# Loading and transposing the first layer's output in bf16 through one PSUM tile

## The reference

```python
x = _layernorm(x + attn(x, Ws, Wa, Wo, bo))
up_gate = einsum('bsd,hd->bsh', x, W1);  up_lin = einsum('bsd,hd->bsh', x, W3)   # d = 2048, h = 8192
hidden  = fwht(silu(up_gate) * up_lin)             # Walsh-Hadamard transform over h
x = _layernorm(x + einsum('bsh,dh->bsd', hidden, W2))
```

## Time and profile before

| | us |
|---|---|
| median of 3 timed runs | 6237.64 |
| fastest and slowest of them | 6152.71, 6242.62 |
| the profiled execution, whole | 5735.62 |
| its span on the slowest core (core 4) | 5734.0 |
| spans of the eight cores | 5688.7 to 5734.0 |

### The profile page before, as it was taken

One profiled execution on the slowest core, in us unless ns is written; L12 is line 12 of the kernel. 1 busy time (PEld: TensorE's weight loads), 2 busy tenths in 40 slices (PEclk: granted clock), 3 DMA queues, 4 the chain that ended last, 5 costly groups with the idle time before them and its releaser, 6 DMA issues.

```text
span 5734.0 us, 46561 instructions; the slowest of 8 cores (5688.7 to 5734.0 us)
## 1 busy us (share of the span) xinstructions
PE 3764.7 (66%) x16956; PEld 1737.1 (30%) x17248; DVE 900.4 (16%) x1961; ACT 494.7 (9%) x688; POOL 233.7 (4%) x384
## 2 busy tenths in 40 slices
PE   1211121455665666569999999999995999149980
PEld 0000000112333333334444444444442444014430
DVE  1211121013333332041111011101110000120003
ACT  1111111000111110000000000000000000010002
POOL 0000000210000000000000000000001000000000
PEclk7555565776777778679999999999997999569995
DMA  9888877664222222343223322233224223542224
GB/s 181 144 154 150 149 147 123 112 107 121 78 89 98 87 83 89 119 153 67 57 56 58 61 57 57 56 58 61 58 56 156 88 88 97 174 162 88 90 79 168
DMA packets 295630, 584.28 MB, mean 102 GB/s; under 512 B 18160, under 2 KB 186352, under 8 KB 280560
## 3 DMA queue, kind: packets, MB, share of 16 engines
q0 software_dynamic: 63312, 270.66, 23.8%
q1 hardware_dynamic: 232096, 310.62, 19.2%
HBM read 583.41 MB, written 167.77 MB: 131 GB/s over the span
## 4 chain that ended last, share of the span: by engine, by line
PE 57%; DMA 27%; DVE 5%; issue 4%; SPq 4%; ACT 1%; another core or an unknown queue 1%; POOL 1%; DVEq 0%; ACTq 0%; POOLq 0%
PE up L649 15%; PE up L660 15%; PE dps L760 13%; DMA vc<-vb 7%; DMA t2sb<-w2tmp 5%; PE av L490 4%; PE sc L558 4%; SPq L256 3%; DMA w2tmp<-t1full 3%; DMA zz<-z2s 3%; DMA w2p<-t2full 2%; DMA zt<-zz 2%; DMA xsb<-xkT 2%; PE pj L353 1%; DMA Hd<-hid 1%
## 5 line engine op out<-in xcount | busy, mean ns | idle before, releaser
L760 PE MATMUL dps<-w2h,Hd 128*128 128x512 bf16 x4014 | 895.5, 382 | 309.0 <-DMA w2h<-w2p 269.0
L649 PE MATMUL up<-y1t,w1b 128*128 128x512 bf16 x4014 | 919.9, 379 | 4.5 <-DVE y1t L628 0.3
L660 PE MATMUL up<-y1t,w3b 128*128 128x512 bf16 x4014 | 919.9, 379 | 4.3
L760 PEld LDWEIGHTS dps<-w2h,Hd 128*128 128x128 bf16 x4096 | 401.7, 98 | 802.8 <-issue 331.4
L490 PE MATMUL av<-PT,vc 128*128 128x256 bf16 x2304 | 413.1, 341 | 274.2 <-DMA vc<-vb 255.1
L649 PEld LDWEIGHTS up<-y1t,w1b 128*128 128x128 bf16 x4096 | 400.9, 98 | 483.4 <-issue 0.7
L660 PEld LDWEIGHTS up<-y1t,w3b 128*128 128x128 bf16 x4096 | 400.7, 98 | 483.4
L278 PE MATMUL pt<-t2sb,i2h_bf 128*128 128x512 bf16 x251 | 84.6, 448 | 680.7 <-DMA t2sb<-w2tmp 671.6
L675 DVE TENSOR_TENSOR hstg<-silu,up 128x512 bf16<-128x512 bf16 x256 | 176.1, 688 | 1592.8 <-PE up L660 743.2
L490 PEld LDWEIGHTS av<-PT,vc 128*128 128x128 bf16 x2304 | 252.1, 118 | 417.3 <-issue 351.0
L671 ACT ACTIVATE silu<-up 128x512 bf16<-128x512 f32 x256 | 152.8, 597 | 1607.6 <-PE up L649 1555.1
(11 more groups left out here) (89 smaller groups left out, 1387.0 us busy)
## 6 DMA issues: line engine op xcount, KB each, us to landing
vc<-vb SPq DMA_DIRECT2D x288, 256.0 KB, 2.7
w2h<-w2p POOLq DMA_DIRECT2D x64, 1024.0 KB, 6.6
rhs<-w2ch POOLq DMA_DIRECT2D x8, 4096.0 KB, 42.1
w2tmp<-t1full SPq DMA_DIRECT2D x8, 4096.0 KB, 46.8
t2sb<-w2tmp SPq DMA_DIRECT2D x16, 2048.0 KB, 14.3
w2p<-t2full SPq DMA_DIRECT2D x16, 2048.0 KB, 15.6
w1b<-w1tp POOLq DMA_DIRECT2D x64, 512.0 KB, 6.2
w3b<-w3tp POOLq DMA_DIRECT2D x64, 512.0 KB, 6.8
```

The source lines that it names most:

```text
L649: t.matmul(p1[:], bw1[:, k * 128:(k + 1) * 128], y1t[:, k * TQ + n * 512:k * TQ + n * 512 + 512], start=(k == 0), stop=(k == 15), skip_gro ...
L660: t.matmul(p3[:], bw3[:, k * 128:(k + 1) * 128], y1t[:, k * TQ + n * 512:k * TQ + n * 512 + 512], start=(k == 0), stop=(k == 15), skip_gro ...
L760: t.matmul(dps[dbase + m][:], Hd2[:, hh * FT2 + m * 128:hh * FT2 + (m + 1) * 128], buf[:, h2 * 512:(h2 + 1) * 512], start=(qb == 0 and h2 ...
```

## The change

The loop that builds `y1t` is rewritten. The load goes through GpSimd's queue and not SyncE's, and writes bf16 into the buffers `y1bf` (half the bytes of `y1f`). The transposes read bf16, use `ident_bf`, and all write one new bf16 PSUM tile `trps` of 128x128; the copies read it. The load of tile m + 2 waits for the transposes of tile m (its readers) and no longer for the last copy. The `w1b` and `w3b` loads follow in the same queue behind the 16 loads of y1. Nothing else changes.

```diff
--- before.py
+++ after.py
@@ -602,34 +602,32 @@
             y1t = CB(nc.sbuf_tensor("y1t", [128, 16 * TQ], BF16))
             w1b = [CB(nc.sbuf_tensor(f"w1b{i}", [128, 16 * 128], BF16)) for i in range(2)]
             w3b = [CB(nc.sbuf_tensor(f"w3b{i}", [128, 16 * 128], BF16)) for i in range(2)]
-            y1f = [CB(nc.sbuf_tensor(f"y1f{i}", [128, D], F32)) for i in range(2)]
+            y1bf = [CB(nc.sbuf_tensor(f"y1bf{i}", [128, D], BF16)) for i in range(2)]
             hstg = [CB(nc.sbuf_tensor(f"hstg{i}", [128, 512], BF16)) for i in range(4)]
             silu = [CB(nc.sbuf_tensor(f"silu{i}", [128, 512], BF16)) for i in range(2)]
+            trps = CB(nc.psum_tensor("trps", [128, 128], BF16))
             up = [CB(nc.psum_tensor(f"up{i}", [128, 512], F32)) for i in range(4)]
 
             for m in range(16):
-                buf = y1f[m % 2]
-                E.op("sync",
+                buf = y1bf[m % 2]
+                E.op("gpsimd",
                      (lambda g2, m=m, buf=buf: g2.dma_start(
                          out=buf[:],
                          in_=d_y1[m * 128:(m + 1) * 128, :])),
-                     reads=(f"y1d:{m}", f"y1f{m % 2}"),
-                     writes=(f"y1fW{m % 2}",), dma=f"y1bf{m % 2}")
+                     reads=(f"y1d:{m}",),
+                     writes=(f"y1bf{m % 2}",), dma=f"y1bf{m % 2}")
                 for c in range(16):
-                    tp = up[c % 4][:, 0:128]
                     E.op("tensor",
-                         (lambda t, c=c, buf=buf, tp=tp:
-                          t.transpose(tp, buf[:, c * 128:(c + 1) * 128],
-                                      ident_f32[:])),
-                         reads=(f"y1fW{m % 2}", "ident_f32"),
-                         writes=(f"up{c % 4}",))
+                         (lambda t, c=c, buf=buf, m=m:
+                          t.transpose(trps[:], buf[:, c * 128:(c + 1) * 128],
+                                      ident_bf[:])),
+                         reads=(f"y1bf{m % 2}", "ident_bf"), writes=("trps",))
                     E.op("vector",
-                         (lambda v, c=c, m=m, tp=tp:
+                         (lambda v, c=c, m=m:
                           v.tensor_copy(
                               y1t[:, c * TQ + m * 128:c * TQ + (m + 1) * 128],
-                              tp)),
-                         reads=(f"up{c % 4}",),
-                         writes=((f"y1t:{c}:{m}",) + ((f"y1f{m % 2}",) if c == 15 else ())))
+                              trps[:])),
+                         reads=("trps",), writes=(f"y1t:{c}:{m}",))
             for hc in range(64):
                 bw1, bw3 = w1b[hc % 2], w3b[hc % 2]
                 E.op("gpsimd",
```

## The result

| | before | changed |
|---|---|---|
| median of 10 timed runs each | 6002.01 | 5841.8 |
| least and greatest | 5723.37, 6261.61 | 5832.86, 6352.47 |
| profiled execution | 5735.62 | 5842.04 |
| ratio, first comparison | | 1.0159 (95%: 1.0119 to 1.0198) |
| ratio, timed again beside before (`e10_changed_again`) | | 1.0195 (1.0179 to 1.0211) |

The change makes the kernel 1.6 to 2.0% slower. The predicted time, 6347 us with a range from 6249 to 6385, was wrong: it missed the measured median by 506 us. The predicted difference was 109.8 us; the two profiled executions differ by 106.4. Some executions of either kernel run with the cores of one die, sometimes of both, at a lower granted clock and some per cent longer; the ratios leave them out, and by their times the three runs shown with the kernel before (6152 to 6243 us, against 5723 to 5781 otherwise) were such executions.

What follows compares the result with a forecast made beforehand. It saw no single bound: stages run in turn, so the edited stage counts. First load 0.9, transposes 190.5 - 83.5 and clock 1.9 gave +109.8 us; on 6237.6 that made 6347.4 us, range 6249 to 6385.

Steps and rivals of the forecast that it cites:

- first load, issue to first transpose: Edited stage's start: the GpSimd load lands in a median 5.9 us, so the first transpose starts 0.9 us later.
- round trip: Edited stage: with one PSUM tile TensorE and VectorE take turns, 0.744 us per transpose, read from the attention stage.
- 256 transposes: Edited stage: 256 turns at 0.744 us take 190.5 us in place of 83.5.
- first 16 up matmuls: Up stage's start: after turns at the low clock these take 5.5 us, adding 1.9 us.
- Loads and weights: Edited stage: later y1 loads hidden behind the turns, `w1b` and `w3b` landed before the up stage; costed at nothing.
- The hidden handoff: Rival, edited stage: one PSUM tile costs nothing beyond the copies; -24 us, 6214 us; chance 0.03.
- The stage at full clock: Rival, edited stage: clock stays at 1.00, trip 0.70 us; +97 us, 6334 us; chance 0.09.
- Loads as the limit: Rival, edited stage: landings of 17.6 us on GpSimd's queue set the pace; +153 us, 6391 us; chance 0.06.
- Slower old loads: Rival, stage before the edit: old loads slower in timed runs than in the profile; +43 us, 6280 us; chance 0.05.
- The signs of being right: Stage about 199 us, transposes 0.74 us apart, load waits some 6 us, clock 0.50, first up matmuls 5.5 us.
- The signs of being wrong: Transposes under 0.70 or over 0.80 us apart, load-released transposes, a `w1b` gap before up, later stages changing length.
- slower by over 2%: Whole kernel: chance about 0.33 of a slowdown over 2% (about 125 us); 0.66 for within 2%.

Runs made afterwards that it cites:

- e10_changed_again: The changed kernel itself with no further edit, timed again beside the kernel before; ratio 1.0195 (1.0179 to 1.0211).
- e2: Changed kernel with four bf16 PSUM tiles, each a bank wide, instead of one; shortest execution 5730.14 us, no ratio.
- e1: Changed kernel with two bf16 PSUM tiles, each a bank wide, instead of one; profiled execution 5743.99 us, no ratio.
- e6: Changed kernel, still one PSUM tile, with four load buffers instead of two; shortest execution 5855.27 us, no ratio.
- e7: Changed kernel with an unused matmul of 128x128 by 512 columns behind each transpose; ratio to the kernel before 1.0189 (1.0164 to 1.0214).
- e8: Changed kernel with eight transposes per bank-wide PSUM tile, one copy for the eight, four such tiles, four load buffers; ratio to the kernel before 0.9943.
- e3: Kernel before with its f32 transposes all through one PSUM tile instead of four; ratio to the kernel before 1.0312 (1.0289 to 1.0335).

## Why the prediction was right and wrong

**The base was wrong, and with it the time and the range.** The step that failed is "so I carry it over as it is: 6237.6 + 109.8 = 6347.4 us". The prediction had the 502 us between its profile and the timed median in front of it, noted that no view says where they lie, and then took the timed runs for the kernel's time in all of its cases. The range, 6249 to 6385, thus held only one of two possible bases, though the profile and the spans of all eight cores in it (5688.7 to 5734.0) stood for the other. In its place the runs showed a base of 5723 to 5781 us in the first comparison and of 5724 to 5739 in the second. No trace exists of the three runs that the prediction started from. That of e2 is of an execution nearly as long, 6167.82 us, and shows where such microseconds can lie. On its slowest core (core 6) the up stage, from 2585.3 to 4656.0,

```profile
2585.30:4656.00 2070.70, 2070.70 (x8193) 872.16 (x8192) 175.76 (x258) 154.17 (x257) 65.45 (x124) 0.85 0.25 49
```

takes 2070.7 us at a mean granted clock of 0.85, where in the profile of before (core 4) it takes 1768.2 (2599.3 to 4367.5) at 1.00, as in the earlier trace rows: 302 us, in dense matmuls. What follows it takes 1510 us where before has 1366.5. The stage of the change is 79.5 us on that core and no longer than on the others. What brings the lower clock isn't shown. Taken against the profiled execution, the same sum gives 5735.6 + 109.8 = 5845.4, and the medians measured were 5841.8 and 5845.0.

**The mechanism and the sum were right.** Term by term:

| term | predicted | measured |
|---|---|---|
| first load, issue to first transpose | 5.9 | 5.2 (2504.35 to 2509.56) |
| round trip | 0.744 | 0.74; 0.84 to 0.95 for the first trip and those into a new tile; mean 0.747 |
| 256 transposes | 190.5 | 190.6, first transpose to first up matmul (2509.56 to 2700.20) |
| stage, before to changed, mean core | +107.9 | +106.6, and 0.45 of GpSimd's later start |
| first 16 up matmuls | 5.5 against 3.5 | 4.8 on core 6, 4.7 to 6.0 on the others, against 3.5 |
| whole | +109.8 | +106.4 between the profiles, +111.0 between the means of their eight spans; 1.0195 of 5730 is +112 |

The round trip could be read in advance because the kernel held the same pair of instructions elsewhere with two tiles, and e1 confirms the step from "two tiles, two transposes for each trip" to "one tile, one". Loads and weights cost nothing, as said: e6 shows it for the loads, and for the weights no gap stands before the up stage. Small misses cancel in the 190.5: 16 trips, the first and those into a new tile, are some 0.1 us longer (2 us in all), the others are 0.740 and not 0.744 (1 us less), and the last trip isn't paid whole, since the first up matmul doesn't wait for the last copy (2700.07 to 2700.20). That the sum agrees to 0.2 us is luck; that it agrees to 1% is not.

**The rivals.** The hidden handoff needed trips below 0.32 us, and they are 0.74; TensorE's waits for the copies are gone only where four tiles are there (1.6 us in e2), which is what the 1.7 us of the earlier trace rows had shown and no more. The stage at full clock didn't come about; by e7's trips it would be worth some 13 us. Loads as the limit: from issue to landing they took 5.0 / 5.8 / 7.0 us (least, median, most) on core 6, against the 11.4 at which they would decide. Slower old loads in the timed runs would make the difference 43 us; the lower end of the second ratio, 1.0179, is 103 us and excludes it.

**The signs.** The signs of being right came: a stage of 195.8 us on core 6, trips of 0.74, one load wait, a granted clock of 0.50. From the first up matmul to the end it is 3133.7 us in the mean of the cores against 3129.6, part of it the slower start of the up stage. The signs of being wrong all looked at the stage and what follows it, and none at the base, where the error was. The sum came out at 1.8% of 6237.6 because the base was too large; of 5735.6 it is 1.91%, and the second comparison has 2% inside its interval. The third given to "slower by over 2%" was about right for a difference that close to the bound, though it had been weighed at 1.8%.

## What to carry to other kernels

One PSUM tile between two engines costs the whole round trip for every item, here 0.74 us where the work in it is a transpose of 0.11 (26.9 us for 256 in e8) and a copy of 0.22; two tiles halve it; with four, or with four wide ones of eight transposes and one copy each, the loads set the pace and not the turns. Look for the same pair of instructions elsewhere in the trace, where they follow each other directly: their starts give the trip. When the timed runs stand 9% above the profiled execution, the base is as uncertain as that: forecast the difference, let the range for the time hold both bases, and name a sign that would tell which it is.

## What the runs showed that I had not expected

- TensorE busy for 92% of the time in the records, with a transpose and a matmul of 512 columns in each turn (e7, core 1) left the granted clock at 0.50 for 160 us, while on core 4 the same program had it rise and fall (means of 0.66 to 0.79 over long stretches).
- At the low clock the way from a transpose to its copy is 0.37 us for bf16 (the changed kernel) and 0.55 for f32 (e3); the way back is 0.15 us beyond the end of the copy in both.
- A copy of 128x1024 bf16 out of PSUM took 0.69 us (e8), where eight of 128x128 take 8 x 0.22 = 1.8.
